# ScalarE copies the turned probabilities of three sequences, and the step statements of four engines change places

## The chip, the cores and the metric

The kernel runs on one core of a Trainium2 chip. The metric is the device time of one execution in microseconds, the median over runs of the same program. The core's engines that matter here are TensorE (PE in the profile, matrix products), VectorE (DVE), ScalarE (ACT), GpSimd (POOL), and SyncE (SP, which only issues DMAs here). Each engine works through its own list of instructions in order and waits on semaphores for the others.

## The reference, cut to what matters

A language model in three parts is computed, in float32, on 8 sequences of 256 tokens with 256 features: a tower (embedding and four state space and MLP layers), one attention layer with a distance kernel, and two layers of windowed attention with a gated MLP. The change is in the order of the second and the third part; the copies that it moves are in the third:

```python
def _layer(x, wqkv, qs, ksc, wo, lg, lb, w1, b1, w2, b2):
    q, k, v = split(shift_token(x) @ wqkv)              # 8 heads of 64
    q, k = rotary_xpos(l2norm(q) * qs, l2norm(k) * ksc)
    x = x + local_attention(q, k, v) @ wo               # windows of 128, look back one
    h = layernorm(shift_token(x)) * lg + lb
    a, g = split(h @ w1 + b1)                           # 682 each
    return x + (a * gelu(g)) @ w2 + b2

for l in range(2):
    x = _layer(x, ...)
h = h + x
```

`shift_token` moves the upper half of the features down by one token. A sequence has 256 tokens, so two windows: the first sees 128 keys, the second 256. With 128 rows of queries on the partitions, the probabilities of one head and sequence are thus 128 x 384. They have to be turned (transposed) before they can be multiplied with the values.

## The kernel before, in words

Each product of float32 is made of three matmuls of split numbers (high x high, low x high, high x low), so each operand needs a high copy (mostly ACT, names with `_hi`) and a low rest (DVE or POOL, `_lo`).

The first phase (the tower) ends at about 500 us. The second (`attention_phase`) works on the 8 sequences up to about 668 us, the third (`window_phase`) to the end. The third has M = 16 units: unit m is a sequence of a layer, 0 to 7 for layer 0 and 8 to 15 for layer 1. Both phases are software pipelines written out by hand. Each engine has a function `half(h)`, called for h = 1 to 17 in the third phase (POOL: 0 to 16, one ahead), and in it a fixed list of steps for the units a = h, b = h-1, ... g = h-6. So in the call h, unit a's input is turned, b is projected and rotated, c and d are in their scores and values, e in its output projection, f and g in their MLP. For small h some of these units do not exist and their steps are left out, but those that remain stand in the same order. Nothing but this order and the semaphores decides what runs when; there is no scheduler at run time. A `tail` function, not changed, ends the phase.

The steps by engine, with their lines in the profile:

- PE: `turn_in` L1859, `project` L1873 to L1875 (q, k or v of one token tile), `turn` L1891 (rotated q or k), `scores` L1904/L1907 (a pair of heads), `turn_p` L1914 (one head's probabilities, three 128x128 transposes into the PSUM tile `ps_p`), `values` L1930/L1932 (a pair), `project_out` L1943 to L1945, `turn_normed` L1961, `hidden_in` L1975 to L1977 (6 chunks, gate and input part), `hidden_out` L1987 to L1991.
- DVE: `x0_variance` L2588 to L2597 and `x0_norm` L2607 (first layernorm of two sequences at a time), `split_in` L2612/L2613, `rotate` L2619 to L2631, `clamp` L2639, `inverse_root` L2645 to L2651 (three operations of 128x16, each on the one before), `soft` L2661/L2663 (masked scores and their maximum), `inverse_sums` L2668, `turned_p` L2674 (copies `ps_p` to the SBUF slot `pt`, 4 slots), `output_lo` L2679, `add_attention` L2683 (raises the semaphore `x_mid`), `upper_stats` L2690, `norm_stats` L2699, `norm_shift` L2716, `split_normed` L2721, `gated` L2730, `hidden_lo` L2738, `add_output` L2745, and `fills` L2947 to L2950.
- ACT: `squares` L2333, `root` L2338/L2340, `turned` L2350 (rotated and turned q and k from PSUM, `w_qt` and `w_kt`), `probabilities` L2354/L2356 (exp), `output_hi` L2364, `norm` L2370, `affine` L2387/L2388, `gelu` L2401 to L2405, `hidden_hi` L2413, `spread` and `keep_values`, and splits of weights (`hi_qkv`, `hi_o`, `hi_1`, `hi_2`).
- POOL: `add_sin` L2988, `scale_k` L2994, `scale_p` L2999/L3000 (probabilities by their inverse sums), `hidden_lo` L3004, `rstd` L3010, `add_bias` (L3018 in layer 0; two operations, L3020 and L3023, in layer 1), and the low parts of weights (`lo_qkv` L2983, `lo_1` L2978, `lo_2` L2972/L2973, `lo_o` L2968).

A head's probabilities, k in the code (k = 8 m + head), go this way: PE `scores`, DVE `soft`, ACT `probabilities`, DVE `inverse_sums`, POOL `scale_p`, PE `turn_p`, DVE `turned_p`, PE `values`, ACT `output_hi`, DVE `output_lo`. PE's next `turn_p` waits until `ps_p` has been copied. Four banks of PSUM (`ring`) are handed round for all other products. SP copies the upper half of the features of X down by a row by DMA once `x_mid` says that the attention was added; `norm_stats` waits for it.

Of the kernel before, what the change touches and what calls it, by code (L numbers as in the profile page):

```python
# [782 lines left out]
def attention_phase(nc, sems, X, dram, wa, out, raw, qkv, tower):  # L783
# [10 lines left out]
    M = NT // 2  # L794
# [10 lines left out]
    with ExitStack() as ctx:  # L805
# [82 lines left out]
        def tensor(pe):  # L888
# [84 lines left out]
            def half(h, turn_first=None):  # L973
                a, b, c, d = h, h - 1, h - 2, h - 3
# [11 lines left out]
                if real(a):  # L986
                    if real(b):
                        pe.wait_ge(v_done, 2 * b + 1)
                    turn_x(a, 6)
                if real(c):  # L990
# [4 lines left out]
                    distances(c, 2, 0)  # L995
                if real(b):
                    pe.wait_ge(v_done, 2 * b + 2)
                    turn(b, 0, 0, 2)
                if real(c):
                    if real(b):  # L1000
                        pe.wait_ge(qk_read, 2 * b + 2)
                    else:
                        pe.wait_ge(y_added, (c - 2) + 1)
# [39 lines left out]
                if real(d):  # L1043
# [4 lines left out]
                    else:  # L1048
                        pe.wait_ge(y_added, (d - 1) + 1)
# [7 lines left out]
                if turn_first:  # L1057
                    turn_first()
                if real(c):
                    values(c, 2, 2)  # L1060
                if real(a):
# [5 lines left out]
                    project_qk(a, 0, 0)  # L1067
                if real(b):
                    pe.wait_ge(relu_done, 8 * b + 1)
                    distances(b, 1, 3)  # L1070
                if real(c):
                    values(c, 3, 2)
                if real(a):
# [4 lines left out]
                    project_qk(a, 1, 1)  # L1078

# [40 lines left out]
        def scalar(act):  # L1120
# [70 lines left out]
            def half(h, spread_first=None):  # L1191
                a, b, c, d, e, f, g, h = h, h - 1, h - 2, h - 3, h - 4, h - 5, h - 6, h - 7
                parts = range(2 * g, 2 * g + 2)
                if real(h):
                    output_hi(h, 1, 2)
                if real(f):
                    query_hi(f, 0, 0)
                    key_hi(f, 1, 1)
                    square(f, 1, 1)
                    keep_values(f, 0, 3)  # L1200
                    query_hi(f, 1, 1)
# [13 lines left out]
                if real(g):  # L1215
                    kernel_exp(g, 4)
                    kernel_exp(g, 5)
                    kernel_exp(g, 6)
# [3 lines left out]
                if real(g):  # L1222
                    kernel_exp(g, 7)
                    if spread_first:
                        spread_first()
                    output_hi(g, 0, 2)
                if real(f):
                    kernel_exp(f, 0)
                if real(e):
                    square(e, 0, 0)  # L1230
                    key_hi(e, 0, 0)
# [35 lines left out]
        def vector(dve):  # L1267
# [95 lines left out]
            def half(h, norm_first=None):  # L1363
                a, b, c, d, e, f, g = h, h - 1, h - 2, h - 3, h - 4, h - 5, h - 6
# [9 lines left out]
                if norm_first:  # L1374
                    norm_first()
                if real(a):
                    norm_stats(a, 0)
                if real(e):
                    clip(e, 0, 3)
                if real(g):  # L1380
                    add_output(g, 1)
                if real(c):
# [1902 lines left out]
```

## Time and profile before

| what | us |
|---|---|
| median of 3 runs (lowest, highest) | 1275.08 (1273.28, 1277.85) |
| the profiled execution: its time | 1278.31 |
| the profiled execution: its span | 1276.4 |
| PE busy | 1209.8 (95%) |
| DVE busy | 984.7 (77%) |
| ACT busy | 860.2 (67%) |
| POOL busy | 621.2 (49%) |

The profile shows one execution. Its own time is its span and 1.9 us around it. Busy is the time in which an engine had an instruction under way; a matmul's weight load is counted apart. PEclk is the clock that TensorE was granted, as a share of full speed. "A <- B" after a wait means that B's engine released it. A row of a timeline has start, duration, engine, line, operation, out <- in, shapes, count, and in square brackets the idle time ahead of it with what ended it.

### The profile page before, as it was taken

The page shows a single profiled execution, that of the slowest core. Times are in us where ns is not written, and L with a number is a line of the kernel's source. Part 1 is how long each engine was busy: PE and PEld are TensorE (multiplying, and loading weights), DVE is VectorE, ACT ScalarE, POOL GpSimd, SP SyncE. Part 2 cuts the span into 40 slices and gives each one's busy share as a digit, 9 for nine tenths or more (in the row PEclk, how much of TensorE's full clock was granted, in tenths as well). Part 3 has the DMA queues.
Part 4 walks back from the last instruction along what each step waited for, and adds up shares of the span by engine and source line. Part 5 has one row for each costly group of instructions (what it writes and reads, how often), then busy time and mean ns, then how long its engine had stood idle before and what let it go on. Part 6 is the DMA issues. An engine that isn't in the chain of part 4 may idle for free.

```text
span 1276.4 us, 26138 instructions
## 1 busy us (share of the span) xinstructions
PE 1209.8 (95%) x8899; PEld 1028.5 (81%) x8899; DVE 984.7 (77%) x2624; ACT 860.2 (67%) x1989; POOL 621.2 (49%) x678
## 2 busy tenths in 40 slices
PE   5999999999999999799978799999999999999998
PEld 3799988988888989577756567888888888888898
DVE  5767676666667777789878988888888888888754
ACT  2455766675556556689964668778777777777764
POOL 6523441361145243455434568556655567556543
PEclk9899999999999999899989999999999999999999
DMA  7400010001000000300110002000100000000001
GB/s 172 115 2 15 2 66 0 14 33 33 0 8 1 1 1 1 77 10 18 58 54 17 1 5 95 6 5 6 48 3 6 22 6 13 22 17 18 22 10 42
DMA packets 39615, 33.25 MB, mean 26 GB/s; under 512 B 16774, under 2 KB 36178, under 8 KB 39506
## 3 DMA queue, kind: packets, MB, share of 16 engines
q1 hardware_dynamic: 38610, 29.74, 7.7%
q0 software_dynamic: 768, 2.10, 1.0%
q8 instruction: 60, 0.98, 0.3%
q14 instruction: 49, 0.40, 0.1%
q10 hardware_dynamic: 128, 0.04, 0.0%
HBM read 25.84 MB, written 4.19 MB: 24 GB/s over the span
## 4 chain that ended last, share of the span: by engine, by line
PE 45%; DVE 6%; issue 3%; POOL 2%; ACT 2%; DVEq 0%; ACTq 0%; POOLq 0%
PE w_ps_p L1914 3%; PE w_ring L1975 3%; PE w_ring L1976 3%; PE w_ring L1873 3%; PE w_ring L1977 3%; PE w_ring L1875 3%; PE w_ring L1874 3%; PE w_ps_a L1932 2%; PE w_ring L1987 2%; PE a_ps L925 2%; PE w_ps_d L1907 2%; PE w_ps_d L1904 2%; PE w_ring L1891 2%; PE w_ring L1988 2%; PE w_ring L1991 1%
## 5 line engine op out<-in xcount | busy, mean ns | idle before, releaser
L392 ACT ACTIVATE t_gf<-t_ps_f,t_fb_cur 128x512 f32<-128x512 f32 x128 | 87.9, 687 | 159.8 <-PE t_ps_f L298 156.6
L542 DVE TENSOR_TENSOR t_g_lo<-t_gf,t_g_hi 128x512 fp32r<-128x512 f32 x128 | 93.3, 730 | 69.3 <-ACT t_g_hi L394 68.9
L311 PE MATMUL t_ps_o<-t_w_hi,t_g_hi 128*128 128x256 f32 x512 | 144.6, 282 | 0.1
L312 PE MATMUL t_ps_o<-t_w_lo,t_g_hi 128*128 128x256 f32 x512 | 143.0, 279 | 0.0
L313 PE MATMUL t_ps_o<-t_w_hi,t_g_lo 128*128 128x256 f32 x512 | 142.9, 279 | 0.0
L695 POOL TENSOR_TENSOR t_rs<-t_ve,t_neghalf 128x4 f32<-128x4 f32 x32 | 40.9, 1277 | 159.8 <-DVE t_ve L503 158.2
L296 PE MATMUL t_ps_f<-t_nh,t_w_hi 128*128 128x512 f32 x256 | 102.6, 401 | 1.5 <-DVE t_nl L518 0.8
L2988 POOL TENSOR_TENSOR w_m<-w_m 128x512 f32<-128x512 f32 x64 | 84.2, 1316 | 36.9 <-DVE w_m L2631 36.8
L298 PE MATMUL t_ps_f<-t_nl,t_w_hi 128*128 128x512 f32 x256 | 100.3, 392 | 0.0
L297 PE MATMUL t_ps_f<-t_nh,t_w_lo 128*128 128x512 f32 x256 | 100.0, 391 | 0.0
L311 PEld LDWEIGHTS t_ps_o<-t_w_hi,t_g_hi 128*128 128x128 f32 x512 | 96.2, 188 | 4.1 <-issue 0.9
L312 PEld LDWEIGHTS t_ps_o<-t_w_lo,t_g_hi 128*128 128x128 f32 x512 | 96.7, 189 | 2.5
L313 PEld LDWEIGHTS t_ps_o<-t_w_hi,t_g_lo 128*128 128x128 f32 x512 | 96.8, 189 | 0.0
L2674 DVE COPY w_pt<-w_ps_p 128x384 f32<-128x384 f32 x128 | 70.5, 551 | 31.4 <-PE w_ps_p L1914 29.9
L1975 PE MATMUL w_ring<-w_nh,w_w_hi 128*128 128x256 f32 x318 | 93.5, 294 | 0.0
L1976 PE MATMUL w_ring<-w_nh,w_w_lo 128*128 128x256 f32 x318 | 88.8, 279 | 0.0
L1977 PE MATMUL w_ring<-w_nl,w_w_hi 128*128 128x256 f32 x318 | 88.7, 279 | 0.0
L2999 POOL TENSOR_TENSOR w_pr<-w_pr,w_rinv 128x256 f32<-128x256 f32 x64 | 39.3, 614 | 101.0 <-DVE w_rinv L2668 101.0
L1873 PE MATMUL w_ring<-qkv_hi,w_ah 128*128 128x512 f32 x188 | 80.6, 429 | 6.7 <-DVE w_al L2613 5.7
L3004 POOL TENSOR_TENSOR w_h_lo<-w_gate,w_h_hi 128x256 fp32r<-128x256 f32 x75 | 54.6, 737 | 60.1 <-ACT w_h_hi L2413 60.1
L394 ACT ACTIVATE t_g_hi<-t_gf 128x512 fp32r<-128x512 f32 x128 | 80.9, 632 | 4.1
L1178 ACT ACTIVATE a_e<-a_dist,a_gsc 128x384 f32<-128x384 f32 x128 | 70.2, 621 | 8.3 <-DVE a_dist L1336 6.8
(369 smaller groups left out, 4285.0 us busy)
## 6 DMA issues: line engine op xcount, KB each, us to landing
t_raw<-in_L_tok_w SPq DMA_DIRECT2D x8, 1024.0 KB, 5.4
out<-X SPq DMA_DIRECT2D x14, 256.0 KB, 2.2
raw<-in_L_ffn_wqkv SPq DMA_DIRECT2D x2, 1536.0 KB, 6.9
raw<-in_L_ffn_w SPq DMA_DIRECT2D x4, 640.0 KB, 4.8
w_raw_o<-out SPq DMA_DIRECT2D x8, 256.0 KB, 2.8
w_xs<-X SPq DMA_DIRECT2D x14, 127.0 KB
w_raw<-in_L_ffn_w SPq DMA_DIRECT2D x2, 640.0 KB
t_raw_d<-in_L_tok_D SPq DMA_DIRECT2D x4, 256.0 KB
```

The source lines that it names most:

```text
L296: pe.matmul(ps_f[:, j % 2, :], w1_hi[:, c, col], nh[1][:, c, :], start=(c == 0), stop=False)
L297: pe.matmul(ps_f[:, j % 2, :], w1_lo[:, c, col], nh[1][:, c, :], start=False, stop=False)
L298: mm = pe.matmul(ps_f[:, j % 2, :], w1_hi[:, c, col], nl[1][:, c, :], start=False, stop=(c == DC - 1))
L311: pe.matmul(out, g_hi[:, j % 4, tok], w2_hi[:, j, :], start=(j == 0 and t % 2 == 0), stop=False, skip_group_check=True)
L312: pe.matmul(out, g_hi[:, j % 4, tok], w2_lo[:, j, :], start=False, stop=False, skip_group_check=True)
L313: mm = pe.matmul(out, g_lo[:, j % 4, tok], w2_hi[:, j, :], start=False, stop=(j == FC - 1 and t % 2 == 1), skip_group_check=True)
L392: act.activation(gf[:, j % 2, :], ps_f[:, j % 2, :], ACT.Gelu, bias=fb_cur[:, j:j + 1]).then_inc(pf_free, 1)
L542: dve.tensor_tensor(g_lo[:, j % 4, :], gf[:, j % 2, :], g_hi[:, j % 4, :].bitcast(F32), ALU.subtract).then_inc(g_split, 1)
L1873: pe.matmul(ring[:, RB[b], :], ah[:, c, tok], qkv_hi[:, c, cols], start=(c == 0), stop=False)
L1975: pe.matmul(dst, w1_hi[:, c, u, cols], n_hi[:, c, :], start=(j % 2 == 0 and c == 0), stop=False, skip_group_check=True)
L1976: pe.matmul(dst, w1_lo[:, c, u, cols], n_hi[:, c, :], start=False, stop=False, skip_group_check=True)
L1977: mm = pe.matmul(dst, w1_hi[:, c, u, cols], n_lo[:, c, :], start=False, stop=(j == chunks[-1] and c == DC - 1), skip_group_check=True)
```

## The change

In the third phase the copies `turned_p` of the tiles k below `BY_SCALAR = 24` (three sequences, units 0 to 2) are done by ACT and no longer by DVE. Beside that, the lists of `half` of PE, ACT, DVE and POOL are put in another order, in the third phase and in the second. Parentheses around the tuple of units change nothing, and the conditions `h != M + 1` stand in place of the early `return`; branches for units that can't occur are gone. The core of the diff:

```diff
+    BY_SCALAR = 3 * H
...
+            def turned_p(k):                      # ACT
+                if not 0 <= k < BY_SCALAR:
+                    return
+                if k >= PTS:
+                    act.wait_ge(S["pv_done"], (k - PTS) // 2 + 1)
+                act.wait_ge(S["p_full"], k + 1)
+                act.activation(pt[:, k % PTS, :], ps_p[:, 0, 0:SC], ACT.Copy).then_inc(S["pt_done"], 1)
...
             def turned_p(k):                      # DVE
+                if k < BY_SCALAR:
+                    return
```

The new order of the third phase, by engine, in the units a to g of the call; a number is the step's own (head or pair of the unit, chunk of the MLP, or token tile):

```text
PE    hidden_in(g,2) values(d,0) turn_p(d,3) project(b,0,q) turn(c,q,1) project(b,0,k) turn_p(d,4) project(b,1,q)
      turn(c,k,1) [h=1: first_values(0)] values(d,1) turn_p(d,5) hidden_in(g,4) turn(b,q,0) hidden_out(g,0) project(b,1,k)
      scores(c,0) turn_p(d,6) hidden_out(g,1) ... turn_normed(f) hidden_out(g,2) values(d,2) scores(c,1) turn_p(d,7)
      project_out(e) hidden_in(f,0) [h=1: first_values(1)] scores(c,2) values(d,3) turn_p(c,0) (wait x_mid) hidden_in(f,2)
      hidden_in(f,4) hidden_out(g,3) hidden_out(g,4) hidden_out(g,5) project(b,0,v) turn_in(a) hidden_in(f,0,a) turn_p(c,1)
      project(b,1,v) scores(c,3) turn_p(c,2) turn(b,k,0)
DVE   clamp(b,0) norm_shift(f) gated(g,4) gated(g,5) rotate(b,q,1) turned_p(d,6) soft(c,0) soft(c,1) split_normed(f)
      rotate(b,k,1) inverse_sums(c,0) soft(c,2) soft(c,3) turned_p(d,7) output_lo(d,2) inverse_root(b,0) add_attention(e)
      soft(c,4) inverse_sums(c,1) clamp(b,1) hidden_lo(g,5) soft(c,5) upper_stats(e) add_output(g) turned_p(c,0)
      norm_stats(e) turned_p(c,1) gated(f,0) output_lo(d,3) inverse_root(b,1) gated(f,1) soft(c,6) split_in(a)
      turned_p(c,2) inverse_sums(c,2) soft(c,7) gated(f,2) gated(f,3) [h=2: x0_variance(2)] turned_p(c,3) output_lo(c,0)
      rotate(a,q,0) turned_p(c,4) inverse_sums(c,3) rotate(a,k,0) turned_p(c,5) output_lo(c,1)
ACT   output_hi(d,0) probabilities(d,6) turned_p(d,3) squares(b,q,0) probabilities(d,7) turned(c,q,1) squares(b,k,0)
      turned_p(d,4) turned(c,k,1) output_hi(d,1) hidden_hi(g,1) hidden_hi(g,2) squares(b,q,1) turned_p(d,5) norm(f)
      turned(b,q,0) hidden_hi(g,3) turned_p(d,6) affine(f) root(b,0) squares(b,k,1) probabilities(c,0) probabilities(c,1)
      output_hi(d,2) hidden_hi(g,4) hidden_hi(g,5) turned_p(d,7) probabilities(c,2) probabilities(c,3) output_hi(d,3)
      gelu(f,0..5) turned_p(c,0) probabilities(c,4) root(b,1) probabilities(c,5) turned_p(c,1) spread(a,0)
      keep_values(b) hidden_hi(f,0) turned_p(c,2) turned(b,k,0) keep_values(b)
POOL  add_sin(b,k,1) scale_k(b,1) hidden_lo(f,0) scale_p(c,2) add_sin(a,q,0) scale_p(c,3) hidden_lo(f,1) hidden_lo(f,2)
      [h=12: lo_1(1,0)] [h=7: lo_qkv(0)] hidden_lo(f,3) add_sin(a,k,0) add_sin(a,q,1) scale_p(b,0) add_bias(e)
      [h=8: lo_qkv(2)] hidden_lo(f,4) scale_k(a,0) scale_p(b,1) ... rstd(d) [h=7: lo_qkv(1)] [h=12: lo_2(1)]
```

The parts of the diff of `half` that the prediction speaks of most:

```diff
 DVE
                 if real(c):
-                    soft(H * c + 0)
-                    soft(H * c + 1)
...
+                if real(b) and h != M + 1:
+                    inverse_root(b, 0)
                 if real(e):
                     add_attention(e, 0)
-                    upper_stats(e)
...
-                if h == 2:
-                    x0_variance(2)
-                if real(c):
-                    turned_p(H * c + 2)
-                if h == 2:
-                    fills()
...
+                if h == 2 and h != M + 1:
+                    x0_variance(2)
 POOL
-                if h == 8:
-                    lo_qkv(2)
-                if real(c):
-                    scale_p(NU * c + 2)
...
                 if real(e):
                     add_bias(e)
+                if h == 8:
+                    lo_qkv(2)
 PE
+                if real(c):
+                    scores(NU * c + 2)
+                if real(d):
+                    values(NU * d + 3)
+                if real(c):
+                    turn_p(H * c + 0)
+                if real(f):
                     if real(e):
                         pe.wait_ge(S["x_mid"], e + 1)
...
                     hidden_in(f, 2, 1, 0, "g_full")
```

In the second phase PE does one part of the distances ahead of turning the next input, and the last two value products after the projections; ACT makes the high part of the queries and the squares before a high part of the output; DVE adds the output and clips one tile before the statistics of the next input; POOL scales before the root, and makes a part of the third phase's weights later.

## Rows read from the trace of the kernel before

**Rows 1.** Windows: stretch, us, busy of PE PEld DVE ACT POOL, PEclk, DMA share, GB/s.
```profile
510.00:668.00 158.00, 141.01 (x1323) 106.35 (x1321) 134.84 (x307) 129.64 (x270) 72.97 (x102) 0.92 0.15 44
680.00:709.00 29.00, 19.94 (x112) 14.20 (x112) 24.35 (x83) 14.50 (x48) 14.53 (x14) 0.94 0.00 1
709.00:761.00 52.00, 46.79 (x313) 34.05 (x314) 47.23 (x165) 31.57 (x105) 30.44 (x31) 0.97 0.01 4
...
794.00:1205.00 411.00, 406.37 (x3101) 344.30 (x3098) 345.87 (x1046) 305.96 (x860) 246.86 (x255) 1.00 0.05 14
```

**Rows 2.** Waits of PE from 680 to 794 us: total, times, longest.
```profile
PE w_ps_p L1914 <- DVE w_pt L2674: 4.4, 4, 1.7
PE w_ring L1873 <- DVE w_al L2613: 4.1, 2, 3.1
PE w_ps_d L1904 <- ACT w_kt L2350: 2.6, 4, 0.9
PE w_ps_d L1904 <- DVE w_mx L2663: 1.6, 4, 0.7
PE w_ring L1961 <- DVE w_m L2631: 1.2, 1, 1.2
```

**Rows 3.** Lines L2674, L2350, L2364 from 640 to 800: ns min/median/max.
```profile
L2674 DVE COPY w_pt<-w_ps_p x29: 522/551/558, 701.2 to 798.6; 128x384 f32<-128x384 f32 x29
...
L2350 ACT ACTIVATE w_kt<-w_ring x9: 597/597/619, 685.5 to 792.7; 128x512 f32<-128x512 f32 x9
...
L2364 ACT ACTIVATE w_ot_hi<-w_ps_a x13: 362/383/398, 706.7 to 794.3; 128x256 fp32r<-128x256 f32 x13
```

**Rows 4.** Timeline of PE in the opening, the longest wait for a copy.
```profile
723.72 0.30 PE L1914 MATMUL w_ps_p<-w_ident,w_pr 128*128 128x128 f32 x1 [1.69 <-DVE w_pt L2674]
```

**Rows 5.** Timeline of DVE in the opening, the statistics of h = 2.
```profile
704.74 1.39 DVE L2588 BATCH_NORM_STATS2 w_x_st<-X 128x6 f32<-128x256 f32 x4
```

**Rows 6.** Timelines of PE and POOL in the steady stretch.
```profile
902.24 2.40 POOL L2983 TENSOR_TENSOR qkv_lo<-raw,qkv_hi 128x1024 fp32r<-128x1024 f32 x1
...
906.26 0.33 PE L1914 MATMUL w_ps_p<-w_ident,w_pr 128*128 128x128 f32 x1 [1.44 <-POOL w_pr L3000]
...
1082.62 0.44 PE L1932 MATMUL w_ps_a<-w_pt,w_v 128*64 128x256 f32 x2 [1.80 <-issue]
```

**Rows 7.** Timelines of DVE and POOL, small products beside POOL's work.
```profile
1077.18 2.90 DVE L2645 TENSOR_TENSOR w_ya<-w_y 128x16 f32<-128x16 f32 x1
...
1149.57 0.18 DVE L2647 SCALAR_TENSOR_TENSOR w_yb<-w_ya,w_sc 128x16 f32<-128x16 f32 x1
...
1151.93 1.30 POOL L2988 TENSOR_TENSOR w_m<-w_m 128x512 f32<-128x512 f32 x1
...
1152.06 1.20 DVE L2647 SCALAR_TENSOR_TENSOR w_yb<-w_ya,w_sc 128x16 f32<-128x16 f32 x1
```

**Rows 8.** Timeline of PE in a steady half, first rows of four steps.
```profile
878.12 0.60 PE L1961 MATMUL w_ring<-w_ident,w_xn 128*128 128x128 f32 x4
...
879.25 0.28 PE L1943 MATMUL w_ring<-w_wo_hi,w_ot_hi 128*128 128x256 f32 x1
...
882.07 0.65 PE L1932 MATMUL w_ps_a<-w_pt,w_v 128*64 128x256 f32 x4
...
884.04 0.36 PE L1975 MATMUL w_ring<-w_nh,w_w_hi 128*128 128x256 f32 x1
```

**Rows 9.** Timelines of DVE and POOL in that half, and a group of the page.
```profile
878.95 0.69 DVE L2619 TENSOR_REDUCE w_ss<-w_m 128x8 f32<-128x512 f32 x1 [1.30 <-ACT w_m L2333]
...
879.71 1.31 POOL L3018 TENSOR_TENSOR X<-X,w_b_all 128x512 f32<-128x512 f32 x1
...
880.15 0.75 DVE L2631 TENSOR_TENSOR w_m<-w_ring,w_tab 128x256 f32<-128x256 f32 x2
...
883.82 0.68 DVE L2683 TENSOR_TENSOR X<-w_ring,X 128x512 f32<-128x512 f32 x1
...
L3004 POOL TENSOR_TENSOR w_h_lo<-w_gate,w_h_hi 128x256 fp32r<-128x256 f32 x75 | 54.6, 737 | 60.1 <-ACT w_h_hi L2413 60.1
```

More of the change, by code:

```diff
@@ L2176, in half @@
                 if real(g):
-                    hidden_out(g, 3, 1)
+                    hidden_out(g, 2, 1)
+                if real(d):
+                    values(NU * d + 2)
+                if real(c):
+                    scores(NU * c + 1)
+                if real(d):
+                    turn_p(H * d + 7)
+                if h == 2:
+                    pe.wait_ge(S["k_read"], 2 * b + 2)
+                    project(b, 0, 2, 3, "v_full")
                 if real(e):
@@ L2254, in half @@
                     turn_in(a, 0)
-                if real(b) and h > 2:
+                if real(f) and h != M + 1:
+                    if real(g):
+                        pe.wait_ge(S["x_out"], g + 1)
+                    else:
+                        pe.wait_ge(S["k_read"], 2 * b + 1)
+                    hidden_in(f, 0, 0, 1, "a_full")
+                if real(c) and h != M + 1:
+                    turn_p(H * c + 1)
+                if real(b) and h > 2 and h != M + 1:
                     if real(f):
@@ L2527, in half @@
                     probabilities(H * c + 1)
-                if real(b):
-                    root(b, 0)
+                if h == 4 and h != M + 1:
+                    hi_2(0)
+                if real(d):
+                    output_hi(NU * d + 2)
+                if real(g):
+                    hidden_hi(g, 4)
+                    hidden_hi(g, 5)
+                if h == 5:
+                    hi_1(0, 0)
+                turned_p(H * d + 7)
                 if real(c):
@@ L2532, in half @@
                     probabilities(H * c + 3)
+                if real(d) and h != M + 1:
+                    output_hi(NU * d + 3)
+                if h == 1:
+                    spread(1, 0)
                 if real(f):
@@ L2544, in half @@
+                if real(f):
+                    gelu(f, 5, 2)
+                turned_p(H * c + 0)
+                if real(f) and (real(b) or real(c)):
+                    act.preload_act_table_set("natural_log_exp_and_others")
                 if h == 13:
                     hi_2(1)
-                if h == 1:
-                    keep_first(0)
-                    keep_first(1)
-                    spread(1, 0)
+                if real(c):
+                    probabilities(H * c + 4)
                 if real(b):
@@ L2566, in half @@
-                if real(f):
-                    hidden_hi(f, 0)
-                if real(b) and h != 1:
-                    keep_values(b, 1, 2)
-                if h == 8:
-                    hi_qkv(2, "v_full")
-                if real(b):
-                    turned(b, 0, 1, 1)
-                if h == 4:
-                    hi_2(0)
+                if real(c) and h != M + 1:
+                    probabilities(H * c + 5)
+                if h == 1:
+                    keep_first(1)
+                turned_p(H * c + 1)
@@ new lines, in half @@
+                if real(a) and h != 1 and h != M + 1:
+                    spread(a, 0)
+                if real(b) and h != 1 and h != M + 1:
+                    keep_values(b, 0, 3)
+                if real(f) and h != M + 1:
+                    hidden_hi(f, 0)
+                if h == 8 and h != M + 1:
+                    hi_qkv(2, "v_full")
+                if h != M + 1:
+                    turned_p(H * c + 2)
+                if real(b) and h != M + 1:
+                    turned(b, 0, 1, 1)
@@ L2577, in tables @@
+                if real(b) and h != 1 and h != M + 1:
+                    keep_values(b, 1, 2)
             def tables():
@@ L2883, in half @@
+                if h == 1 and h != M + 1:
+                    split_in(a, 0)
+                if real(c) and h != M + 1:
+                    turned_p(H * c + 1)
+                if real(f) and h != M + 1:
+                    gated(f, 0, 1)
+                if real(d) and h != M + 1:
+                    output_lo(NU * d + 3)
+                if real(b) and h != M + 1:
+                    inverse_root(b, 1)
+                if real(f) and h != M + 1:
                     gated(f, 1, 1)
-                if h == 1:
+                if real(c) and h != M + 1:
+                    soft(H * c + 6)
```

437 lines of the change are left out of this document (187 added, 250 removed).

## The prediction

> **What bounds the kernel now.** I read first the mean clock and the table by stretch [rows 1], then PE's waits in the opening of the third phase [rows 2], then single rows around them. TensorE sets the end: from 794 to 1205 us it is busy 406 of 411 us, at full clock, so this steady stretch has under 5 us of holes to give. The holes are in two places. The second phase (510 to 668) has PE busy 141 of 158 us, DVE 135 and ACT 130: three engines are tight together. The opening of the third phase has PE busy 19.9 of 29.0 us (680 to 709) and 46.8 of 52.0 (709 to 761) [rows 1]. There the order of each engine's statements was laid out for the steady half, while no older unit yet fills the gaps. The waits [rows 2] name who is late: the copy of the turned probabilities on DVE (4.4 us in 4 waits), the low part of the first input on DVE (4.1 in 2), the turned keys on ACT (2.6 in 4), the masked scores on DVE (1.6 in 4), a rotation on DVE (1.2).
>
> **Part 1: the copies go to ScalarE.** DVE loses 24 copies of 128x384, ACT gains 24. On DVE one lasts 551 ns, and the next instruction starts some 0.47 us after it began [rows 3]. ACT has never done this shape: from PSUM, 128x256 takes it 383 ns and 128x512 takes 597 ns [rows 3], so 384 columns lie between, and I take the middle, 0.49. The sum on an engine's queue: DVE -24 x 0.47 = -11.3 us, ACT +24 x 0.49 = +11.8 us. (By "ScalarE: Activation LUTs", section on what ACT_TABLE_LOAD costs, the Trainium skill has an ACTIVATE with immediates at 186 ns + 0.833 ns per column, an estimate of 506 ns here; the same sum.) Both are spread over halves h = 2 to 5, where ACT has room: 14.5 of 29 us and 31.6 of 52 busy [rows 1]. What PE gets of it is the 4 waits for `w_pt`. The largest [rows 4] is 1.69 us at 723.72, because on DVE the copy stands in line behind other work; with ACT idle it comes about as PE's result lands. I count 3.8 of the 4.4 us. That PE stood still there also cost clock: the granted clock of 709 to 761 is 0.97 [rows 1], 0.03 x 52 = 1.6 us, all behind that wait; I count it as gone. The masked scores then come earlier on a DVE with 11 us less: half of their 1.6, 0.8. The turned keys on ACT (2.6) could get worse by the copies ahead of them or better by their new place; 0, with 1 us to either side.
>
> **Part 2: DVE's order in h = 2.** The statistics of the second sequence (4 instructions in 1.39 us from 704.74, [rows 5]) and what follows stood before the split of the input for the next unit. Of PE's two waits for a split (4.1 us, the longer 3.1, [rows 2]) the shorter, 1.0, is that one. The statistics now come behind the last masked scores: 0.9 saved, as something else will be late by 0.1. The other wait (3.1) stays: what feeds it is the same chain of work. Rotation before the turned normed rows, 1.2 [rows 2]: `split_normed` now comes before the last rotation, so some returns; 0.9. **Opening in all: 3.8 + 1.6 + 0.8 + 0.9 + 0.9 = -8.0 us.** Bounds: 0 (each wait is replaced by the next) and -11 (all waits of DVE's, 4.4 + 1.0 + 1.6 + 1.2, and clock, with 1 us of the keys).
>
> **Part 3: the steady halves, what goes.** PE waited 1.44 us at 906.26 for scaled probabilities [rows 6], because a low-part split of 2.40 us (902.24) stood ahead of them on POOL, [rows 6]. This split (`lo_qkv(2)`) now comes after `add_bias`. -1.44, taken as -1.5. The hole of 1.80 at 1082.62 [rows 6] stays: `lo_2(1)` is still in h = 12, now nearly last, where it can hold the same two small operations of `inverse_root`, a wash.
>
> **Part 4: the steady halves, what comes.** Here is the risk. Two rows first. DVE's small product of 128x16 lasts 0.17 to 0.18 us unhindered (1149.57), but 1.20 (1152.06) and 2.90 us (1077.18) while POOL runs an SBUF to SBUF operation; it ends when POOL's does [rows 7]. The DVE instructions held are those that have both inputs in SBUF; those that read PSUM go on. "SBUF — State Buffer", section "SBUF: two separate sides", in the Trainium skill says that the shared port pair is an exclusive lock, taken for a whole instruction by a POOL operation or a DVE operation with two SBUF inputs, and the loser waits; the trace agrees, 2.90 us for what takes 0.18. Without the lock the sum of this part is 0, with it up to +14.5 (below).
>
> In the new order DVE does `inverse_root(b,0)` ahead of `add_attention(e)`, and PE's `hidden_in(f,2)` waits for the latter (`x_mid`). From the start of PE's `turn_normed`: that and `hidden_out` take 1.13 us (878.12 to 879.25), `project_out` 2.82 (to 882.07), values, scores and `turn_p` 1.97 (to 884.04) [rows 8], and `hidden_in(f,0)`, 12 matmuls at the 0.118 us of those of `project_out`, 1.42. Behind these stand another values, scores and `turn_p`, 1.97: PE wants x_mid at 9.3. ACT and DVE, an estimate by the order of their statements: ACT does four affine operations at 0.45 (to 2.5), the root and the squares (to 3.5); DVE the rotation (878.95 to 880.90, 1.95, [rows 9]) to 5.5, then two masked scores, the copy of 0.47 and `output_lo`, 2.2 together, to 7.7, `inverse_root` (three at 0.17) to 8.2, `add_attention` 0.68 [rows 9] to 8.9. So there is a slack of 0.4 to 0.5 us if nothing holds DVE. But POOL, from 5.6, does `scale_p` (1.65), `add_bias` (1.31 [rows 9]; in layer 1 two of them) and `hidden_lo` (0.74 [rows 9]) without a gap: to 8.6, then 9.3. If the three small operations, each depending on the one before, are caught behind each, `add_attention` ends at 10.2 in layer 0 and 11.4 in layer 1: PE stalls 0.85 and 2.1 us. Halves with units e, f and g or c all live are h = 5 to 11 (7 in layer 0) and 12 to 15 (4 in layer 1): 7 x 0.85 + 4 x 2.1 = 14.4. It needs three orders to fall within a few tenths, and DVE gets its turn between two POOL operations, as the row of 0.18 beside the one of 1.20 shows: so 0 to 14.5. I take 0.4 in each of 11 halves, **+4.5**, nearer to the lower end.
>
> **Part 5: all other moves** (PE's `turn_p`, values, scores a few matmuls earlier or later; ACT's `hi_` splits; POOL's rotations; gelu) at nothing. What hides them is that TensorE's queue holds the same matmuls, 99% busy, and the waits for ACT and POOL have 1 to 3 us of other PE work before them; if this cover is gone, one stall of 0.5 us in 11 halves is 5 us. SP's statements are the same and none of the moved functions issues a DMA; the one that copies X's upper half down by a row waits for x_mid and moves with it, at most by part 4's times, and its reader, `norm_stats`, now stands behind two masked scores and more. In the second phase PE has 17 us idle of 158, DVE 23, ACT 28 [rows 1]; moved are `turn_x`, `values` and ACT's query copies by less than a microsecond each. 8 halves by 0.5 us either way, +-4; I take 0.
>
> **Sum.** -8.0 - 1.5 + 4.5 + 0 = -5.0. The profiled run was 1278.3 us (span 1276.4), 3.2 above the median of 1275.1, so I make 1273.3 for such a run and 1270 for the median.
>
> **Rivals.**
> *Slower: the lock at x_mid.* Everything of part 4 falls as in the full count: -8 - 1.5 + 14.5 = +5, time 1280. For it: rows of 1.20 and 2.90; POOL busy 247 of 411 us [rows 1]. Against it: slack 0.45 and DVE is served between two POOL operations. It decides from the point where the held `inverse_root` ends later than 8.7 us after `turn_normed`'s start, that is where it is held over 0.5 us; the whole gain is eaten at 0.86 us of stall in each of 11 halves.
> *Nothing comes of it: the wait moves.* ACT's copy stands before the turned keys and probabilities, so PE waits for `w_kt` instead of `w_pt`. The opening gives 2 instead of 8: -2 - 1.5 + 4.5 = +1, time 1276. For it: keys are already 2.6 us of waits [rows 2]. Against it: ACT is half idle there.
> *More: no lock reaches PE.* -9.5, time 1265.5. For it: the slack is positive by each row taken alone.
> That the change doesn't do what it says: DVE's function returns for the same k for which ACT's doesn't, so no copy is doubled or lost; no chance of its own.
>
> **How the numbers follow.** Forecast 0.35, lock 0.30, moved wait 0.17, more 0.18. About what a measurement can tell from no change is 0.3%, 3.8 us: faster is under 1271.3, slower over 1278.9. Of the forecast's 0.35, 0.25 lies faster, 0.08 within and 0.02 slower; of the lock's, 0.03 within and 0.27 slower; of the moved wait's, 0.01, 0.12 and 0.04; "more" is 0.18 faster. Together: faster 0.44, same 0.23, slower 0.33. Range 1262 to 1283: it holds the lock's time with 3 us of the second phase's bound, and "more" with as much. As the cases have both signs: the forecast's own range is 1266 to 1274.
>
> **What would show it.** PE's waits from 680 to 794: `w_ps_p L1914` under 1 us (part 1), the second `w_al` wait gone (part 2), `w_kt` not above 3.6. The granted clock of the stretch that was 709 to 761 at 0.99 or more. ACT's copy at 0.44 to 0.55. The distance between the starts of halves in steady state: 35.7 us as before, or up to 36.5 (layer 0) and 37.8 (layer 1) with PE waiting at L1975 for DVE's X, with `inverse_root` rows over 0.5 us. The second phase the same length within 4 us. Wrong makes me: a second phase that moves by more, or PE waits in the steady halves at another place than x_mid.

## The result: 3.6% slower, and the profile after

The changed kernel takes 1321.74 us (median of 4 runs, 1318.98 to 1323.29), the kernel before 1276.03 (4 runs). The ratio is 1.036, 95% interval 1.033 to 1.039. That is 45.7 us slower than the kernel before. The forecast was 1270, the range 1262 to 1283: the time lies outside the range and far beyond the slower rival's 1280.

The page of the profile of the changed kernel, its parts 1 and 4: busy times, then the chain of work that ended last.

```profile
span 1319.4 us, 26137 instructions
PE 1216.8 (92%) x8899; PEld 1029.6 (78%) x8899; DVE 976.8 (74%) x2600; ACT 868.6 (66%) x2013; POOL 620.1 (47%) x678
...
PE 28%; DVE 15%; DMA 8%; issue 4%; ACT 3%; POOL 1%; SPq 1%; DVEq 0%; POOLq 0%; ACTq 0%
DMA w_xs<-X 8%; PE w_ps_p L1918 2%; PE w_ring L1877 2%; PE w_ring L1895 2%; PE w_ring L1879 2%; PE w_ring L1878 2%; DVE a_dist L1337 2%; PE w_ps_a L1936 2%; DVE w_ya L2657 2%; PE w_ring L1979 1%; PE w_ring L1980 1%; PE w_ring L1981 1%; PE a_ps L925 1%; DVE w_ss L2631 1%; PE w_ring L1991 1%
```

Each engine does the same work as before. PE is busy 1217 us, 1210 before, so some 36 of the 43 us of span are waiting and 7 are the same matmuls taking longer. From the fourth to the fourteenth `add_attention` of the third phase (846.55 to 1203.3 us before, 858.4 to 1246 now) the granted clock was 1.00 before and is 0.98 now: PE is busy 357.4 us instead of 352.1 and stands 30.2 instead of 4.6. So a lower clock comes on top of the waits; no run parts the two. A DMA that was nowhere in the chain before, `w_xs<-X`, is now its costliest line: 8% of 1319 us. It is the copy of X's upper half one row down (the function `shift` in SP's list: one DMA for 127 of the 128 partitions, and behind it one for the single row that crosses from one token tile to the next). Lines have moved by a few: L1914 is now L1918, L1891 is L1895, L1975 is L1979, L2683 is L2697 and L2699 is L2713.

PE's waits from 500 us to the end of the changed kernel (total, times, longest), the first four:

```profile
PE w_ring L1895 <- DVE w_gate L2744: 27.5, 12, 5.3
PE w_ring L1979 <- DVE X L2697: 7.4, 11, 2.4
PE a_ps L938 <- DVE a_dist L1337: 5.6, 6, 1.4
PE w_ps_p L1918 <- DVE w_pt L2688: 5.5, 5, 2.1
```

The first two are not in the kernel before at all. L1979 is the wait for `x_mid` of the prediction's slower rival, 7.4 us. The larger one, 27.5 us, is the last step of PE's half, `turn(b,k,0)`, which waits until chunk 1 of the MLP is gated. It is 1.3 to 1.8 us in nine halves, and 5.3, 3.5 and 5.1 (at 794.64, 911.32 and 1111.32) in the three in which POOL splits weights behind `rstd`: `lo_2(0)`, `lo_qkv(1)` and `lo_2(1)`. DVE's longest wait says why it is late (from 668 us on):

```profile
DVE w_st L2713 <- DMA w_xs<-X: 40.9, 14, 6.8
```

One half shows it whole; it is one of those three, with `lo_qkv(1)` on POOL from 907.05 to 909.40. This is the chain of waits of the changed kernel from 895 to 912 us (start, us, what):

```profile
895.96 0.70 DVE X L2697
896.65 0.02 issue
896.67 0.71 SPq L1779
897.38 0.04 issue
897.42 7.84 DMA w_xs<-X
905.26 0.02 issue
905.28 0.04 DVE w_st L2713
...
907.15 0.33 DVE w_ot_lo L2693
907.48 1.97 DVE w_ya L2657
909.45 0.02 issue
909.47 1.20 DVE w_yb L2659
...
910.78 0.49 DVE w_gate L2744
911.27 0.04 issue
911.32 0.69 PE w_ring L1895 x2
```

`add_attention` starts at 895.96, and `norm_stats` can begin 9.3 us later. DVE had reached it after 6.9 and stood 2.4 us. The 7.84 us in the chain are not all flight. SP's own timeline of these microseconds has both DMAs of `shift`:

```profile
896.67 0.71 SPq L1779 DMA_DIRECT2D w_xs<-X  x1
897.42 4.60 SPq L1780 DMA_DIRECT2D w_xs<-X  x1
```

The second one, 512 bytes, keeps SP's queue busy for 4.60 us, and the reader starts 3.26 us after that. In the 14 halves of the changed kernel the second took 4.5 to 5.9 us, and the reader began 3.2 to 3.6 us after its end each time. Why the second takes so long, and which of the two lands last, is not shown; no run changed either.

Behind `norm_stats` come a copy, a gate, `output_lo`, the three small operations of `inverse_root(b,1)`, here held by POOL (1.97 and 1.20 us for what takes 0.17 [rows 7]; in the halves without a split on POOL only the first is held, 0.96 us), and only then the gate that PE waits for. In the kernel before, `norm_stats` began 12.4 us after `add_attention` in 11 of 14 halves, and DVE's waits for the DMA were 1.1 us in all. A steady half before is 35.6 us from one `add_attention` to the next; in the changed kernel it is 37.6 (858.36 to 895.96), and 43.3 in the next one, with POOL's `lo_qkv(1)` and `lo_qkv(2)`.

### The profile page after: what moved, and what is told of

It is laid out like the page before. It is cut to its first block, busy times and chain, and to the rows that moved or that the text cites. A ratio compares the mean times of both kernels' runs of the same rounds, so it can differ in the third digit from the quotient of the medians.

```text
span 1319.4 us, 26137 instructions
## 1 busy us (share of the span) xinstructions
PE 1216.8 (92%) x8899; PEld 1029.6 (78%) x8899; DVE 976.8 (74%) x2600; ACT 868.6 (66%) x2013; POOL 620.1 (47%) x678
## 4 chain that ended last, share of the span: by engine, by line
PE 28%; DVE 15%; DMA 8%; issue 4%; ACT 3%; POOL 1%; SPq 1%; DVEq 0%; POOLq 0%; ACTq 0%
DMA w_xs<-X 8%; PE w_ps_p L1918 2%; PE w_ring L1877 2%; PE w_ring L1895 2%; PE w_ring L1879 2%; PE w_ring L1878 2%; DVE a_dist L1337 2%; PE w_ps_a L1936 2%; DVE w_ya L2657 2%; PE w_ring L1979 1%; PE w_ring L1980 1%; PE w_ring L1981 1%; PE a_ps L925 1%; DVE w_ss L2631 1%; PE w_ring L1991 1%
## 5 line engine op out<-in xcount | busy, mean ns | idle before, releaser
L2990 POOL TENSOR_TENSOR w_m<-w_m 128x512 f32<-128x512 f32 x64 | 81.4, 1279 | 71.3 <-DVE w_m L2643 71.3
L1979 PE MATMUL w_ring<-w_nh,w_w_hi 128*128 128x256 f32 x318 | 96.5, 304 | 7.4 <-DVE X L2697 7.4
L1879 PE MATMUL w_ring<-qkv_hi,w_al 128*128 128x512 f32 x188 | 75.2, 400 | 0.0
L1878 PE MATMUL w_ring<-qkv_lo,w_ah 128*128 128x512 f32 x188 | 75.0, 399 | 0.0
L1918 PE MATMUL w_ps_p<-w_ident,w_pr 128*128 128x128 f32 x384 | 68.6, 288 | 5.8 <-DVE w_pt L2688 5.5
L1479 POOL TENSOR_SCALAR_AFFINE_SELECT a_e<-a_e 128x512 f32<-128x512 f32 x64 | 41.6, 653 | 67.2 <-ACT a_e L1178 67.1
```

The lines of the kernel that those rows point to most:

```text
L1878: pe.matmul(ring[:, RB[b], :], ah[:, c, tok], qkv_lo[:, c, cols], start=False, stop=False)
L1879: mm = pe.matmul(ring[:, RB[b], :], al[:, c, tok], qkv_hi[:, c, cols], start=False, stop=(c == DC - 1))
L1979: pe.matmul(dst, w1_hi[:, c, u, cols], n_hi[:, c, :], start=(j % 2 == 0 and c == 0), stop=False, skip_group_check=True)
```

## The experiments

All medians are beside the kernel before on the same chip (1275.0 to 1276.3 us over the sets). Twelve kernels were run. **Theory:** `norm_stats` stands inside the flight of the DMA. **Rivals:** the port lock ahead of `x_mid`; the copies; the second phase.

**norm_late.** DVE's order of the changed kernel:

```diff
-                if real(e) and h != M + 1:
-                    norm_stats(e)
...
                 if real(f) and h != M + 1:
                     gated(f, 1, 1)
+                if real(e) and h != M + 1:
+                    norm_stats(e)
```

> The changed kernel with one step moved: DVE's norm_stats(e), which reads the rows that a DMA copies one row down, goes from behind turned_p(c,0) to behind gated(f,1). Theory (the DMA in flight): in the changed kernel norm_stats is reached 6.9 us after add_attention, the shifted rows land after 9.3, so DVE stands 2.4 us in 13 of the 14 halves and PE pays for it at turn(b,k,0), which waits for gated(f,1), 1.4 us each time. Moved, the distance is over 9 us: DVE's wait for w_xs falls from 40.9 to under 8 us, PE's wait for w_gate from 27.5 to under 10, the time from 1322 to 1300 (1293 to 1308). Rival (the port lock on inverse_root sets the half): the wait for w_xs goes too, but PE gets the gate no earlier than inverse_root(b,1) allows, and the time stays within 4 us of 1322.

Measured 1299.0 us, ratio 1.016 (1.013 to 1.020): 22.7 less than the changed kernel, by one step moved past five others. DVE's wait for `w_xs` is 7.6 us in 3 times (40.9 in 14), the waits of PE for the gate are gone from the list, the 7.3 us at L1979 remain. The theory's number held. The move takes two things from ahead of the gate, the wait and the 0.9 us of `norm_stats`' own work. The rows say which one counts. In a steady half of this run the next copy, `turned_p(c,1)`, starts 9.27 us after `add_attention`, when PE's result is there; DVE has stood 2.4 us for it. `norm_stats` would fit into that gap if its rows were there at 6.9. They come at 9.3, so in the changed kernel the copy starts at 10.25. No run moved the DMA alone.

**root0_late.**

```diff
-                if real(b) and h != M + 1:
-                    inverse_root(b, 0)
                 if real(e):
                     add_attention(e, 0)
+                if real(b) and h != M + 1:
+                    inverse_root(b, 0)
```

> The changed kernel with inverse_root(b,0) put behind add_attention(e), where it was ahead of it. Its three small operations take 1.5 to 3.8 us in the changed kernel where 0.58 is the unhindered time. Theory (the lock stands ahead of x_mid, as in the slower rival of the prediction): PE's 7.4 us of waits at the hidden_in behind x_mid go, and x_mid comes 1.5 to 2.3 us earlier in each of 11 halves, so that the shifted rows land as much earlier, while norm_stats stays where it was in time: the DMA wait falls from 2.4 to about 0.7 us each. Time 1300 (1292 to 1306). Rival (the lock costs only what PE waits for x_mid): 1322 - 7 = 1315 (1312 to 1318).

Measured 1308.35, ratio 1.026 (1.023 to 1.029), 13.4 less than the changed kernel, between the two expectations. PE's waits at L1979 are gone and its waits for the gate 20.5 us instead of 27.5, but the DMA wait stayed at 38.9 us in 14. Two things make up this sum. In most halves up to 1045 us it fell from 2.4 to between 1.1 and 1.4 us; 0.7 was expected. From 1078 on it rose from 2.6 to between 3.3 and 3.6: SP's first DMA of `shift` began 2.8 us after `add_attention` there and not 0.7, since a load stands ahead of it in SP's list that waits for POOL's `add_bias`. In the half from 926.85, where SP had loads of weights to issue first, it began 5.4 us after, and DVE waited 7.2. So `add_attention` came earlier, but there SP could not use it.

**order_only.** `BY_SCALAR = 0 * H`.

> The changed kernel with BY_SCALAR = 0: all orders as changed, every copy of turned probabilities on DVE. Theory (the copies are worth what the prediction gave them, in the opening only): 3.8 us of waits for w_pt and some clock come back, 1322 + 4 to 8 = 1326 to 1330, all of the difference before 795 us. Rival (the DMA wait swallows it, since DVE stands anyway): 1322, within 2 us.

Measured 1330.05, ratio 1.042 (1.040 to 1.045): the copies on ScalarE are worth 8.3 us within the new order, the upper end of the theory. (PE is busy 7.0 us longer in this trace, 1223.8 against 1216.8, at a mean granted clock of 0.972 against 0.981; the copies' own waits and the lower clock behind them can't be told apart in the 8.3.) From each trace's first `turn_in` to the first `add_attention` it is 87.9 us (662.37 to 750.26) against 81.6 with the copies (660.98 to 742.56), so 6.3 of it come there.

**copies_only.** The kernel before with the 24 copies on ScalarE (`turned_p` as in the change, its calls put into ScalarE's old list, for instance):

```diff
                 if real(c):
                     probabilities(H * c + 4)
+                turned_p(H * c + 0)
```

> The kernel before, in its own orders, with only the 24 copies of units 0 to 2 on ScalarE, each behind a step of the same time in ScalarE's list. Theory (part 1 of the prediction): the waits of PE for w_pt from 680 to 794 fall from 4.4 to about 1 us, time 1276 - 4 = 1272 (1269 to 1274). Rival (the wait moves to ScalarE's turned keys or is replaced by the next): 1276, within 2 us.

Measured 1274.9, ratio 0.9995 (0.997 to 1.002): no change that can be told. PE's waits from 680 to 794 in this kernel:

```profile
PE w_ps_p L1915 <- ACT w_pt L2366: 8.2, 9, 1.7
PE w_ps_d L1905 <- ACT w_kt L2351: 2.8, 4, 0.9
PE w_ps_d L1905 <- DVE w_mx L2680: 1.3, 3, 0.7
```

Against [rows 2], the wait for the copy moved from DVE to ACT and grew from 4.4 to 8.2 us. In an order not fitted to them, the copies are worth nothing: the rival of the moved wait, by a wait for the copy itself and not for the keys. So part 1 of the prediction depends on the order it is put in.

**both_late.** Both moves together.

> The changed kernel with both moves of the first set: inverse_root(b,0) behind add_attention(e) and norm_stats(e) behind gated(f,1). Theory (two separate losses: the shifted rows in flight, 23 us by norm_late, and the lock ahead of x_mid, 7.3 us of waits at L1979 that norm_late still had): 1299 - 7 = 1292 (1288 to 1296), no wait at L1979, DVE's wait for w_xs under 8 us. Rival (the lock only moves to where the rotated scores wait for inverse_root): 1299, within 3 us.

Measured 1289.7, ratio 1.012 (1.008 to 1.016), within the theory: 9.3 less than norm_late by the medians. The two intervals overlap a little (norm_late's began at 1.013), so the size is loose; root0_late, clear of the changed kernel, says the same. The lock ahead of `x_mid` is a loss of its own. No wait at L1979 is left. As in norm_late, PE now waits for scaled probabilities (`w_pr` of POOL, 10.4 us in 4; 10.5 there).

**norm_early.** The suspected loss added to the kernel before:

```diff
                     inverse_sums(NU * c + 1)
+                if real(e) and h != M + 1:
+                    norm_stats(e)
+                if real(c):
                     turned_p(H * c + 0)
...
-                if real(e):
-                    norm_stats(e)
```

> The kernel before with one step moved, to add the suspected loss by itself: DVE's norm_stats(e) goes from behind turned_p(c,1) and inverse_root(b,0) to ahead of turned_p(c,0), where DVE reaches it 7.4 us after add_attention by the trace of before, while the shifted rows have landed 9.3 us after it in the changed kernel. Theory (the DMA in flight): DVE waits 1.9 us for w_xs in 13 halves, 25 us in all; PE wants turned_p(c,0) and the gate soon behind and pays for half to all of it: 1276 + 12 to 25 = 1288 to 1301. Rival (DVE has the slack in its own order, the damage of the changed kernel came from all moves together): 1276, within 4 us.

Measured 1298.0, ratio 1.017 (1.014 to 1.021): 23.0 us slower than the kernel before from one step, within the theory's range. But the loss is not the one that the theory describes. DVE's waits for the DMA are 11.4 us in 14, not 25: 3.1, 2.0 and 2.9 in three halves, and 0.2 to 0.6 in the other eleven. A steady half (idle time and its releaser in brackets):

```profile
969.33 0.69 DVE L2683 TENSOR_TENSOR X<-w_ring,X 128x512 f32<-128x512 f32 x1 [0.31 <-PE w_ring L1945]
...
978.67 0.49 DVE L2699 BATCH_NORM_STATS2 w_st<-w_xs 128x6 f32<-128x128 f32 x2 [0.24 <-DMA w_xs<-X]
979.20 0.28 DVE L2705 BATCH_NORM_AGGREGATE w_mv<-w_st 128x2 f32<-128x12 f32 x2
979.51 0.64 DVE L2710 TENSOR_SCALAR w_ve<-w_mv 128x2 f32<-128x2 f32 x1
980.06 0.55 DVE L2674 COPY w_pt<-w_ps_p 128x384 f32<-128x384 f32 x1
```

`norm_stats` begins 9.3 us after `add_attention`, as in the changed kernel, but DVE had only just got there. The 7.4 us that I gave for this place are true of one half in the trace of before (883.82 to 891.21); in the other steady ones it is 9.0. The copy behind it starts 10.7 us after `add_attention`, where it was 9.0:

```profile
955.12 0.69 DVE L2683 TENSOR_TENSOR X<-w_ring,X 128x512 f32<-128x512 f32 x1 [0.31 <-PE w_ring L1945]
...
964.14 0.53 DVE L2674 COPY w_pt<-w_ps_p 128x384 f32<-128x384 f32 x1
...
967.57 0.48 DVE L2699 BATCH_NORM_STATS2 w_st<-w_xs 128x6 f32<-128x128 f32 x2
```

Of these 1.7 us, 0.24 are the DMA and 1.4 are `norm_stats`' own three operations. PE pays at this copy, `w_pt`, 19.6 us in 19 waits where the kernel before had 4.5: 0.5 in each steady half, and 3.8, 1.8 and 2.7 in the three in which DVE waited 2 to 3 us for the DMA. So the DMA shows in those three, and elsewhere the work of `norm_stats` at a bad place. The run is no second measure of the DMA's cost, and nothing ties its 23.0 to the 22.7.

**phase2_only.** The kernel before with the second phase's new order.

> The kernel before with only the second phase's new order. Theory (part 5 of the prediction): the same within 4 us, 1276 (1272 to 1280). Rival (the new order of the second phase is part of the loss): 1280 or more, with a phase from 512 to the last output projection (671 before) that is longer by the same amount.

Measured 1275.8, ratio 1.0003 (0.999 to 1.002): nothing, as forecast.

**splits_early.** both_late, and on POOL:

```diff
+                if h == 7:
+                    lo_qkv(1)
+                if h == 12:
+                    lo_2(1)
+                if real(b) and h == 4:
+                    lo_2(0)
                 if real(d) and h != M:
                     rstd(d)
```

(with the same statements taken out behind it)

> both_late with POOL's weight splits lo_qkv(1), lo_2(0) and lo_2(1) ahead of rstd(d) where they were behind it. In norm_late POOL stood 5.9 to 9.1 us before rstd, waiting for norm_stats, and did the splits of 2.4 to 3.7 us only then, ahead of scale_p(c,2), for which PE waited 3.2, 2.0 and 3.2 us. Theory (the splits are late because rstd holds the queue): these three waits go, 8 us less than both_late: 1284 (1280 to 1288). Rival (the late scale_p comes from the late norm_stats alone): as both_late, within 3 us.

Measured 1281.6, ratio 1.004 (1.003 to 1.006): 8.1 less, as expected. PE's waits for POOL's scaled probabilities fell from 10.4 to 2.1 us. POOL's `rstd` waits for `norm_stats`, so what stands behind `rstd` pays for the late statistics a second time. In the changed kernel itself PE has no wait for scaled probabilities; there the three late splits show as the three long waits for the gate, since they hold the `inverse_root(b,1)` ahead of it.

**norm_later.** splits_early with `norm_stats(e)` moved once more, behind `soft(c,7)`.

> splits_early with norm_stats(e) moved on once more, from behind gated(f,1) to behind soft(c,7), past soft(c,6), split_in(a), turned_p(c,2) and an inverse of sums. splits_early still had three halves in which the shifted rows were not there in time (DVE waits 10.3 us in 3 times), and behind them PE waits of 3.2 us for w_al at 755, 2.7 for w_pt at 936 and 2.3 at 1219. Theory (the rest of the loss is the same DMA in the same three halves): these fall, 1281.6 - 6 = 1275.5 (1272 to 1279). Rival (POOL pays: its rstd waits for norm_stats, and rotation, scale_k and scale_p(c,2) stand behind it, so PE waits for w_pr instead): no gain or a loss, 1281 to 1300.

Measured 1312.1, ratio 1.028 (1.026 to 1.031): 30.5 us more, the rival, and beyond it. PE's first wait, and POOL's:

```profile
PE w_ps_p L1918 <- POOL w_pr L3002: 32.7, 13, 3.9
...
POOL w_rs L3012 <- DVE w_ve L2724: 119.6, 15, 11.6
```

And one half of POOL's timeline:

```profile
946.87 0.71 POOL L3012 TENSOR_TENSOR w_rs<-w_ve,w_neghalf 128x2 f32<-128x2 f32 x1 [9.67 <-DVE w_ve L2724]
...
950.61 0.62 POOL L3001 TENSOR_TENSOR w_pr<-w_pr,w_rinv 128x256 f32<-128x256 f32 x1
951.18 1.04 POOL L3002 TENSOR_TENSOR w_pr<-w_pr,w_rinv 128x512 f32<-128x512 f32 x1
```

POOL stands 9.67 us for `rstd`, and has 4.7 us of its own work behind it before the probabilities are scaled. `norm_stats` has a window: ahead of it the DMA holds DVE, behind it POOL stands.

**rstd_later.** norm_later, and POOL's `rstd` for that unit goes past the work that was held behind it:

```diff
                 if real(c):
                     scale_p(NU * c + 2)
+                if real(e):
+                    rstd(e)
...
-                if real(d) and h != M:
-                    rstd(d)
```

> norm_later with POOL's rstd for the same unit moved from the end of its half to behind scale_p(c,2) of the next, 4 us of POOL's own work later, so that POOL doesn't stand for norm_stats. If the rival of norm_later holds, this takes its loss away and gives 1275.5 (1272 to 1279); if the theory holds, it is as norm_later, within 3 us. If norm_shift on DVE, which waits for rstd, then comes late, PE's turn_normed waits (over 0.3 us at L1965 in the steady halves) and the time is 1280 or more.

Measured 1273.4, ratio 0.9998 (0.997 to 1.002): level with the kernel before. So moves of four kinds of step (`norm_stats`, `inverse_root(b,0)`, the three weight splits against `rstd`, `rstd` itself) give back 48 us of medians, as much as the whole loss. That is a balance: `norm_stats` and `rstd` now stand where neither kernel had them, and PE still has waits that the kernel before lacks (3.7 us for turned keys from POOL, 4.4 for a copy at 784). That nothing else in the change costs anything is not shown. Part of the balance is clock: PE is busy 1204.1 us here and 1216.8 in the changed kernel, at mean clocks of 0.988 and 0.981.

**copies_split.** copies_only, and POOL's `lo_qkv(2)` behind `add_bias(e)`.

> The kernel before with the two parts of the change that alone looked harmless: the 24 copies on ScalarE as in copies_only (1274.9, 1.0 below before) and POOL's lo_qkv(2) behind add_bias, where its 2.4 us no longer stand ahead of scale_p for which PE waited 1.4 us (part 3 of the prediction). Theory: that wait goes: 1275 - 1.0 - 1.5 = 1272.5 (1270.5 to 1274.5). Rival (the split of 2.4 us holds DVE or POOL's next scale_p at its new place): 1275 or more, with a new PE wait of over 1 us in h = 8 (880 to 925).

Measured 1273.2, ratio 0.9989 (0.997 to 1.0006): not told from no change. In its trace the wait of 1.44 us [rows 6] is gone and no new one stands in h = 8, so part 3 of the prediction was right in that order.

**three_placed.** rstd_later with two more steps of DVE moved:

```diff
-                if h == 5:
-                    x0_variance(3)
...
                     gated(f, 1, 1)
+                if real(b) and h != M + 1:
+                    inverse_root(b, 1)
...
+                if h == 5:
+                    x0_variance(3)
```

(the second behind `gated(f,3)`; `inverse_root(b,1)` is taken out ahead of `gated(f,1)`)

> rstd_later with two more moves on DVE, away from places where POOL's weight splits hold small operations with a PE wait behind them: x0_variance(3) from ahead of soft(c,5) to behind gated(f,3) in h = 5 (one operation of 128x4 took 4.6 us beside lo_2(0), and PE waited 4.4 for the copy behind it at 784), and inverse_root(b,1) from ahead of gated(f,1) to behind it (its first operation took 3.0 us beside lo_2(1), and PE waited 2.5 for the gate at 1075). Theory (each lock costs PE what stands behind it in DVE's list): 1273.4 - 6 = 1267.5 (1265 to 1270), under the kernel before by 0.5%. Rival (the lock is paid at the next place, the rotated scores or the next gate): 1272 or more.

Measured 1273.6 beside 1276.3 for the kernel before: ratio 0.9973 (0.9957 to 0.9989). It is the only kernel of the twelve whose interval lies under one, by 0.3% and barely, so it is weak evidence of a gain; against rstd_later, whose interval overlaps, nothing is shown. The wait of 4.4 us at 784 is gone and the 2.5 us at 1075 are 1.4 and 0.6, but the wait for the rotation at L1965 grew from 2.6 to 3.6, and the expected 6 us did not come.

## Why the prediction was wrong, point by point

**The step that failed** is the sentence of part 5 on the DMA: it "waits for x_mid and moves with it, at most by part 4's times, and its reader, norm_stats, now stands behind two masked scores and more", priced at nothing. I named the DMA and its reader and never laid them on a time line. In the changed order the reader is reached 6.9 us after `add_attention` instead of 12.4; the DMA takes 9.3. The rows to see it were in the trace of before. In its timeline of DVE, the third phase's first `add_attention` and its reader stand 9.5 us apart, with a wait for the DMA of half a microsecond; in the steady halves they stand 12.4 apart with none (955.12 and 967.57 above):

```profile
748.09 0.69 DVE L2683 TENSOR_TENSOR X<-w_ring,X 128x512 f32<-128x512 f32 x1 [0.16 <-PE w_ring L1945]
...
757.56 0.49 DVE L2699 BATCH_NORM_STATS2 w_st<-w_xs 128x6 f32<-128x128 f32 x2 [0.52 <-DMA w_xs<-X]
```

norm_late shows its worth, 22.7 us, half of the loss. Behind it hangs POOL's `rstd`, and behind that POOL's splits, which the change had also moved there from ahead of it: 8.1 us more (splits_early, measured in the order of both_late). The prediction spoke of one of them, `lo_2(1)`, as a wash, and of `lo_qkv(1)` and `lo_2(0)` not at all.

**Part 4, the lock at x_mid**: the mechanism and the place were right. PE waited at L1979 for X in 11 halves, and the `inverse_root(b,0)` ahead of it was held. The time line held too: in a steady half POOL's `scale_p` began 5.6 us after `turn_normed` (849.11 to 854.67), as forecast. The size was not right: the operations took 1.5 to 1.8 us in layer 0 and 2.3 in layer 1 (0.58 unhindered), PE saw only 0.25 and 0.8 of it, 7.4 us with one of 2.35 in the half of `lo_qkv(2)`, against the 4.5 that I took and the 14.4 of the full count. But what PE waits is not its worth: moved away it gave 9.3 (both_late) to 13.4 us (root0_late), since DVE is late by the whole hold for all that follows. That DVE "gets its turn between two POOL operations" did not hold either: at 1105.98 in the changed kernel the first small operation took 4.46 us, across three POOL operations.

**Part 1, the copies**: ScalarE's copy lasts 491 ns, as estimated (0.49), 24 times:

```profile
L2361 ACT ACTIVATE w_pt<-w_ps_p x24: 463/491/532, 696.8 to 775.6; 128x384 f32<-128x384 f32 x24
```

In the changed kernel PE's waits for `w_pt` from 680 to 794 fell from 4.4 to 1.4 us, and the copies' worth in that order, 8.3 us, is the size forecast for the opening. What I had wrong is what it is counted from: order_only is 8.3 slower than the changed kernel, not the kernel before 8 slower than it. At the second `add_attention` of the third phase the changed kernel was no longer ahead (777.64; 776.44 before), because the first wait for the DMA, 6.8 us, falls into the opening. (In rstd_later this wait is 0.8 us and the first two `add_attention` stand 28.3 us apart, as before; here they stand 35.1 apart.)

**Part 2**: the waits of PE for `w_al` fell from three of 5.7 us to one of 1.6, more than forecast. The rotation ahead of L1965 grew from 1.2 to 2.6 us where I had 0.9 saved. The granted clock did not rise to 0.99. Windows of the changed kernel (columns as in [rows 1]):

```profile
680.00:709.00 29.00, 26.43 (x150) 19.31 (x149) 23.63 (x86) 18.82 (x60) 15.37 (x16) 0.90 0.00 1
709.00:761.00 52.00, 45.12 (x294) 33.03 (x293) 37.73 (x141) 38.35 (x122) 28.99 (x30) 0.93 0.01 4
761.00:794.00 33.00, 24.28 (x183) 18.97 (x181) 28.62 (x70) 23.05 (x62) 22.23 (x17) 0.97 0.16 53
```

0.90 and 0.93 stand where [rows 1] has 0.94 and 0.97, and in the first stretch PE was even busier (26.4 us of 29, 19.9 before). What sets the clock in these stretches is not shown. That I counted 1.6 us of clock as gone because a wait goes was not earned.

**Part 3**: right for the hole at 906 in the order of before (copies_split). In the changed kernel `lo_qkv(2)`, at 936.27, holds `inverse_root(b,0)` for 3.75 us, and PE waits 2.35 for `x_mid` at 940, so more came than went. The 3.47 at 911 belong to `lo_qkv(1)`. `lo_2(1)` was no wash: held beside it, `inverse_root(b,1)` took 4.9 us with the gate behind it, and PE waited 5.05 at 1111.

**The second phase**: nothing, as forecast (phase2_only).

**The rivals and the range**: the slower rival had the right sign and one of the right mechanisms at 0.30; none had the DMA. All cases ran along waits that the trace of before showed for PE, and so none could reach 1322. A range from such cases alone is too narrow where four hand-made orders are changed at once.

## What to carry to other kernels

Where steps are moved in an in-order list, lay out for each semaphore from a DMA the time from the step that starts it to the step that reads it, before and after: here 12.4 us became 6.9 against 9.3 from trigger to reader, which costs nothing in the trace of before, and 22.7 us came back when the step was moved away. Look there also at what stands ahead of the DMA in the issuing engine's own list (root0_late). When a step is moved to test a wait, subtract the step's own work from the result (norm_early). A step that another engine waits for has a window, with an early and a late edge; the late one is found at the first consumer's own list (POOL's `rstd` ahead of `scale_p`). An offload is worth what the order around it lets through: the same 24 copies gave 8.3 us in one order and nothing in the other.

## What the runs showed of the hardware

The copy of 127 KB and one row within the core's own memory, started by a semaphore from DVE, took 9.3 us from the start of the DVE operation to its reader in the steady halves: 0.7 for the DVE operation, 0.71 for the first DMA on SP's queue, 4.60 for the second, of 512 bytes, and 3.26 to the reader. The DMA share from 895 to 912 is 0.03; as it is a mean over 16 engines, it says nothing on how busy the one or the few were that moved the rows. It took 11.6 (939.25 to 950.80 in the changed kernel) where SP was issuing loads of weights just ahead of it: the first DMA then began 1.6 us after `add_attention`, and the second took 5.90. Beside a POOL operation DVE is also held in operations with only one tensor input: in rstd_later a bound of 128x16 took 2.85 us and an addition of a constant to 128x4 values took 4.59 while POOL split weights.

```profile
772.90 2.85 DVE L2651 TENSOR_SCALAR w_sc<-w_ss 128x16 f32<-128x16 f32 x1
...
777.51 4.59 DVE L2609 TENSOR_SCALAR w_x_ve<-w_x_mv 128x4 f32<-128x4 f32 x1
```

The prediction had the lock only for operations with two inputs in SBUF, and had DVE served between two POOL operations. The second of these rows was not: it ran from 777.51 to 782.10 across the three POOL operations that began at 777.26, 777.95 and 780.82.
